# A deformable-convolution block on one core: the half-partition shift of the sampled rows, issued by GpSimd instead of by the sync engine

## What is computed

```python
x = x + _L0_conv_ref(_gn(x), ...)   # offsets, bilinear sampling, 3x3 convolution
x = x + _L1_conv_ref(_gn(x), ...)   # a depthwise 3x3 convolution whose taps come from the image's mean
```

## Time and profile before

| what | value |
|---|---|
| median of 3 runs | 1491.65 us |
| the profiled execution, its own time | 1493.54 us |
| its span, first to last instruction | 1491.7 us |
| TensorE busy (matmul) | 1436.3 us, 96% of the span |
| VectorE busy | 1257.4 us, 84% |
| ScalarE busy | 1152.9 us, 77% |
| GpSimd busy | 437.1 us, 29%, 474 instructions |
| mean granted TensorE clock | 0.992 |
| mean DMA rate | 207 GB/s |

### The profile page before, as it was taken

One profiled execution on the slowest core, in us unless ns is written; L12 is line 12 of the kernel. 1 busy time (PEld: TensorE's weight loads), 2 busy tenths in 40 slices (PEclk: granted clock), 3 DMA queues, 4 the chain that ended last, 5 costly groups with the idle time before them and its releaser, 6 DMA issues.

```text
span 1491.7 us, 30369 instructions
## 1 busy us (share of the span) xinstructions
PE 1436.3 (96%) x12300; PEld 617.9 (41%) x12300; DVE 1257.4 (84%) x884; ACT 1152.9 (77%) x1970; POOL 437.1 (29%) x474
## 2 busy tenths in 40 slices
PE   5898798999999999999999999999999999999978
PEld 2333343444444444444444444444444444444433
DVE  4999999988888898889888988888888889888900
ACT  6789687986888778887888877888688877766643
POOL 5000734225050432306141151412505043230120
PEclk9999999999999999999999999999999999999999
DMA  8576587977888788886979778897888877767558
GB/s 270 159 191 170 146 215 182 242 197 204 236 224 217 198 213 228 228 216 179 244 206 255 189 206 230 223 233 194 205 236 224 217 199 180 198 179 201 140 145 260
DMA packets 226907, 308.77 MB, mean 207 GB/s; under 512 B 17216, under 2 KB 169152, under 8 KB 226768
## 3 DMA queue, kind: packets, MB, share of 16 engines
q1 hardware_dynamic: 211360, 266.68, 61.2%
q0 software_dynamic: 15408, 40.15, 17.3%
HBM read 190.35 MB, written 38.14 MB: 153 GB/s over the span
## 4 chain that ended last, share of the span: by engine, by line
PE 89%; DVE 4%; DMA 2%; issue 2%; ACT 2%; POOL 1%; SPq 0%; DVEq 0%; ACTq 0%; POOLq 0%
PE z L402 46%; PE dc L442 24%; PE dw L475 14%; PE z L475 3%; DMA yr<-in_planes 1%; DVE nb L840 1%; DVE nb L838 1%; DMA yh<-yr 1%; DVE nb L818 1%; DVE nb L835 0%; PE dc L451 0%; ACT nb L635 0%; DVE nb L844 0%; DVE nb L842 0%; PE z L494 0%
## 5 line engine op out<-in xcount | busy, mean ns | idle before, releaser
L402 PE MATMUL z<-xv,wos 128*64 128x384 f32 x4608 | 766.1, 488 | 10.7 <-issue 7.6
L402 PEld LDWEIGHTS z<-xv,wos 128*64 128x64 f32 x4608 | 330.7, 137 | 429.8 <-issue 428.6
L442 PE MATMUL dc<-sr,wds 128*32 128x384 f32 x2304 | 396.4, 489 | 13.4 <-issue 9.5
L442 PE MATMUL dc<-sh,wds 128*32 128x384 f32 x2304 | 396.4, 489 | 0.0
L1017 POOL DMA_DIRECT2D yr<-in_xr x96 | 86.2, 898 | 767.1 <-ACT yr L669 767.1
L818 DVE COPY_PREDICATED nb<-mu,xv 128x2280 f32<-128x2280 uint16 x96 | 269.2, 2804 | 36.9 <-ACT mu L621 36.5
L442 PEld LDWEIGHTS dc<-sr,wds 128*32 128x32 f32 x2304 | 133.5, 108 | 237.2 <-issue 237.1
L475 PE MATMUL dw<-yh,wy 128*64 128x388 f32 x616 | 229.7, 494 | 0.0
L475 PE MATMUL dw<-yr,wy 128*64 128x388 f32 x616 | 229.7, 494 | 0.0
L635 ACT ACTIVATE nb<-xv 128x2292 f32<-128x2292 f32 x96 | 202.9, 2113 | 28.8 <-DVE sr L851 20.6
L614 ACT ACTIVATE du<-z,ob 128x768 f32<-128x768 f32 x96 | 86.4, 900 | 128.8 <-PE z L402 128.2
(11 more groups left out here) (130 smaller groups left out, 1594.6 us busy)
## 6 DMA issues: line engine op xcount, KB each, us to landing
xv<-in_x SPq DMA_DIRECT2D x272, 384.0 KB, 5.6
yr<-in_xr POOLq DMA_DIRECT2D x96, 392.0 KB, 5.0
out<-ot SPq DMA_DIRECT2D x96, 388.0 KB, 3.9
yh<-yr SPq DMA_DIRECT2D x178, 196.0 KB, 3.9
st<-in_planes SPq DMA_DIRECT2D x56, 576.0 KB, 7.5
sh<-sr SPq DMA_DIRECT2D x160, 194.0 KB, 5.1
sh<-sr SPq DMA_DIRECT2D x32, 145.5 KB, 5.7
yr<-in_planes SPq DMA_DIRECT2D x8, 576.0 KB, 10.3
```

Of the source, the lines that this page charges most:

```text
L402: last = nc.tensor.matmul(acc[m], weights[:, kx, :], view[:, :, kx:kx + W], start=kx == 0, stop=kx == 2)
L442: last = nc.tensor.matmul(dc[m, q, 0:NB * PAIRS], weights[:, kx, q], view[:, :, cols], start=first, stop=final)
```

## The change

`s_shift` moves, line for line, from the sync engine's program to GpSimd's; every `sp.` in it becomes `pool.`. In step i it is called behind `add_residual(i - 4)` and ahead of everything else that GpSimd does in the step. The last one, `s_shift(LAST)`, stands between the residuals of chunks 92 and 93. Transfers, sizes, semaphores and waited values are the same.

```diff
-            def s_shift(n):
...
-                sp.wait_ge(sampled, n + 1)
...
-                if i:
-                    s_shift(i - 1)
                 if b + 1 < B and o < STILES:
                     st_load(b + 1, o)
...
-            s_shift(LAST)
...
+            def s_shift(n):
+                b, j = divmod(n, CHUNKS)
+                k, done = s_at(n), s_sh[n % SS]
+                pool.wait_ge(sampled, n + 1)
+                pool.wait_ge(s_pads, SS * b + min(j + 1, SS))
+                wait(pool, dcn_mm, 2 * (n - 2))
+                lo, hi = slice(0, P // 2), slice(P // 2, P)
+                pool.dma_start(sh[lo, k:k + NB, :], sr[hi, k:k + NB, :]).then_inc(done, 16)
...
+                elif k == 0:
+                    pool.dma_start(sh[hi, SS * NB - 1, :], sr[lo, 0, :]).then_inc(done, 16)
+                    pool.dma_start(sh[hi, 0:NB - 1, :], sr[lo, 1:NB, :]).then_inc(done, 16)
+                else:
+                    pool.dma_start(sh[hi, k - 1:k + NB - 1, :], sr[lo, k:k + NB, :]).then_inc(done, 16)
...
                 if i > DCN_STEP:
                     add_residual(i - DCN_STEP - 1)
+                if i:
+                    s_shift(i - 1)
                 if o == 0:
...
-            for n in range(LAST - DCN_STEP, TOTAL):
+            add_residual(LAST - DCN_STEP)
+            s_shift(LAST)
+            for n in range(LAST - DCN_STEP + 1, TOTAL):
                 add_residual(n)
```

More of the change, by code:

```diff
@@ L305, in st_load @@
                 sp.dma_start(st[i % 2][:], planes[b, i]).then_inc(st_in[i % 2], 16)
-            def s_shift(n):
-                b, j = divmod(n, CHUNKS)
-                k, done = s_at(n), s_sh[n % SS]
-                sp.wait_ge(sampled, n + 1)
[L311 to L327, removed]
             def y_shift(n):
@@ L1011, in y_weights @@
                    tap[:].unsqueeze(2).to_broadcast([P, TAPS, CQ]), ALU.mult).then_inc(wy_ok, 1)
+            def s_shift(n):
[6 more added lines that the diff above has]
+                pool.dma_start(sh[lo, k:k + NB, :], sr[hi, k:k + NB, :]).then_inc(done, 16)
+                if j == 0:
+                    pool.dma_start(se[hi, b % 2, :], sr[lo, k, :]).then_inc(se_in[b % 2], 16)
+                    pool.dma_start(fe[2 * C:3 * C, b % 2, :], sr[0:C, k, :]).then_inc(done, 16)
+                    pool.dma_start(sh[hi, k:k + NB - 1, :], sr[lo, k + 1:k + NB, :]).then_inc(done, 16)
+                elif k == 0:
[3 more added lines that the diff above has]
+                    pool.dma_start(sh[hi, k - 1:k + NB - 1, :], sr[lo, k:k + NB, :]).then_inc(done, 16)
+                if j == CHUNKS - 1:
+                    pool.wait_ge(se_in[b % 2], 16 * (b // 2 + 1))
+                    pool.dma_start(sh[hi, k + NB - 1, :], se[hi, b % 2, :]).then_inc(done, 16)
+                    pool.dma_start(fe[C:2 * C, b % 2, :], sr[P - C:P, k + NB - 1, :]).then_inc(done, 16)
             def add_residual(n):
```

## The result

The changed kernel takes **1538.38 us** (median of 4 runs, 1537.56 to 1539.45); the kernel before took 1492.28 beside it. The ratio is 1.0307, with an interval from 1.0291 to 1.0322: 46.1 us slower. 1524.0 was forecast, within 1502 to 1540.

What follows compares the result with a forecast made beforehand. TensorE, busy nearly throughout, was taken as the bound, so each new wait on GpSimd's small arithmetic is lost time. 15.3 + 3.0 + 14.4 = 32.7 us more gave 1524 us, range 1502 to 1540.

Steps and rivals of the forecast that it cites:

- steps 10 and 16: `x_norm` of the second image and `y_norm` of the first: `hidden` of the first image comes 15.3 us later.
- step 18, `y_weights`: `y_weights` of the first image, behind `blend(17)` and two transfers: 3.0 us, bounds 0 and 4.8.
- six times `y_norm`: `y_norm` in images 3 to 8: `hidden` waits 2.4 us each time, 14.4 us in all; bounds 0.5 and 4.2 each.
- the clock: TensorE's granted clock behind the waits of steps 10 and 16: same loss on both sides, plus or minus 2 us.
- places put at 0: `x_norm` and `y_weights` of later images and the edge transfers: covered by about half a step, so 0 us.
- one turn more: Upper bound at `y_weights` of the first image: GpSimd's arithmetic waits out one further VectorE instruction, 4.8 us.
- so the price of issuing does not matter: Images 3 to 8: three transfers are through at 771.3, inside line 818, which runs until 772.45.
- rival 1: Images 3 to 8: GpSimd slips through VectorE's pauses, 0.5 us per image instead of 2.4; 1513 us, chance 0.22.
- GpSimd at its own pace: GpSimd's arithmetic, started late, is not held up by VectorE; 1492 us, no change, chance 0.08.
- the later images do not stall: Same claim as rival 1: 0.5 us per image instead of 2.4 in images 3 to 8; 1513 us, chance 0.22.
- Descriptors held up, too: Each shift transfer on GpSimd also waits for one VectorE instruction; 95.7 us more, 1587 us, chance 0.08.
- Faster: Shifts may land sooner from GpSimd's queue, and TensorE's 3.9 us of waits for them go; 1488 us, chance 0.04.

Runs made afterwards that it cites:

- Experiment 1: The changed kernel with the shift issued by GpSimd behind everything else in its step; 1496.77 us, ratio 1.0038.
- experiment 6: The changed kernel with four products of zeros on TensorE ahead of `hidden` in the six later images; 1532.92 us, ratio 1.0267.
- Experiment 2: The kernel before, shift still on SP, with only the wait for the sampled rows added on GpSimd behind the residual; 1518.50 us, ratio 1.0176.
- Experiments 3: The changed kernel with the shift behind `y_norm` in the fifth step of each image, from the second image on; 1525.62 us, ratio 1.0224.
- 4: The changed kernel with the shift behind `x_norm` and the next chunk's pads at o = 10; 1537.88 us, ratio 1.0311.
- 10: GpSimd issues shifts last in the step (at o = 4 right behind `y_norm`), but the last shift is given back to SP; 1495.82 us, ratio 1.0017.
- 9: GpSimd issues shifts last in the step (at o = 4 right behind `y_norm`), with chunk 93's residual ahead of the last shift; 1500.49 us, ratio 1.0051.
- experiment 7: The changed kernel with the shift last in GpSimd's step, but at o = 4 right behind `y_norm`, ahead of the pads; 1497.29 us, ratio 1.0031.

## Why the prediction was right, and where it fell short

**Right: the mechanism.** The change costs GpSimd little and puts a wait ahead of small arithmetic that TensorE and VectorE want. Experiment 1 shows it with the same transfers and the same wait, and nothing left to stand behind them in the step; the timelines show one operation per VectorE instruction in step 10 and in five of the six later images. Term by term, the forecast beside the trace (waits less those of the earlier trace rows):

| term | forecast | measured, from |
|---|---|---|
| steps 10 and 16 | 15.3 (its rows give 15.2) | 15.8: (16.2 - 7.6) + (11.8 - 4.6) |
| step 18, `y_weights` | 3.0 | 4.7, the wait at `y_bias` |
| six times `y_norm` | 14.4 | 12.0: five of 2.3, one of 0.5 |
| the clock | 0, plus or minus 2 | 9.4: 1071.8 - 1062.4, images 3 to 8 |
| places put at 0, the tail | 0 | 2.4: 44.7 - 42.3 |
| sum | 32.7 | 44.3, of 44.7 in the span |

The two terms of the first image's places leave out two things that nearly cancel. Up to the end of `blend(23)` TensorE is busy for 315.6 us instead of 312.8, 2.8 more, and its waits for shifted tiles are 2.7 us shorter.

**Mis-sized: the clock.** The text had "adds no third of that length, so I take the same loss on both sides, plus or minus 2 us". It looked only at waits as long as those of the earlier trace rows. The runs show that 2.3 us of idling are enough, in four of five images. From n = 23 to 95 the same instructions take 9.4 us more, and experiment 6, which keeps TensorE busy, leaves 0.7 of them; that 0.7 stays open. That 1538.4 still lies in the range, below 1540, is luck in this term: the top was room kept for other terms, 25.2 us for `y_norm` alone, which took 12.0.

**Step 18** came out at its upper bound, "one turn more". Line 978 of GpSimd, and VectorE beside it:

```profile
288.29 2.03 POOL L978 TENSOR_SCALAR tap<-tap,ry 128x16 f32<-128x16 f32 x1
```

```profile
288.26 1.07 DVE L800 COPY_PREDICATED xv<-mv,xv 128x768 f32<-128x768 uint16 x1
289.22 1.00 DVE L801 COPY_PREDICATED nb<-mv,nb 128x768 f32<-128x768 uint16 x1
```

Line 801 begins before line 800 is shown to end, and the operation waits out both: 290.32 against 290.22. This is not a rule. The same two lines stand as close in step 40 (line 800 until 620.39, line 801 from 620.28), and there line 940 ends between their ends, at 620.78. What decided it in step 18 is not shown.

**Right by an argument that was too coarse: "so the price of issuing does not matter"**, said of images 3 to 8. Between my two bounds, 0.63 and 0.95 us, it does not. Experiment 2 shows that at no price at all the first operations of `y_norm` slip in ahead of line 818 and the waits all but vanish, so rival 1 would have come true there. In the changed kernel it did come true in the last of the six images, with 0.5 us.

**The places put at 0** (edges, `x_weights`) did not show in the changed kernel. Experiments 3, 4 and 10 show that they were covered narrowly: when an earlier wait goes, they are next. **The tail** was not costed: the last shift moved ahead of a residual, and the forecast had no term for that.

**The rivals.** *GpSimd at its own pace* falls with step 10's timeline, *the later images do not stall* with the five waits of 2.3 us. *Descriptors held up, too* falls with the 0.53 us between transfers beside line 793 (163.25, 163.78, 164.29). The Trainium skill's rule behind it (SBUF — State Buffer, SBUF: two separate sides) speaks of a VectorE instruction that holds both ports; as far as these transfers go, no run here shows one. *Faster* was wrong on the total but right that waits for shifted tiles would shrink, from 13.4 us to 8.2. The prediction read only 3.9 us as such waits, because the profile puts the others down to "issue". What shrank them is not shown; a shorter landing it is not, as the page's transfers by line show, which answer to the earlier trace rows:

```profile
sh<-sr POOLq DMA_DIRECT2D x160, 194.0 KB, 6.3
```

## What to carry to other kernels

A transfer that is cheap to issue can still be expensive to move: list what stands behind its wait on the new engine, and who waits for each of those. When one place is mended, ask which wait was hidden by it, for here the next one took over four times (experiments 1, 3, 4 and 9). And a TensorE that is busy all the time should be costed with more than its idle time: read the granted clock behind each new wait.

## What the runs showed of the hardware

- 2.3 us of idling, after more than a hundred microseconds without any, were followed by the 1.2 GHz level in four of five images, and so were the 2.8 and 2.9 us in the tails of experiment 7 and the changed kernel. The kernel before idled 2.5 us in its tail, from 1423.07 on, with the clock at 1.00 behind it (1425 to 1432), and in experiment 2, with waits of 0.5 us at most in these images, the clock stayed at 1.00 behind those at 445, 623 and 801 us. With TensorE kept at work by products that nobody uses, it stayed at 1.00, and the kernel was 5.5 us faster.
- A shift takes 6.3 us to land in the changed kernel and 5.1 in the kernel before, but it is not GpSimd's queue in itself that makes it late: from the same queue, at a later place in the step, it takes 4.7 us in experiment 1, 4.5 in experiments 7 and 9 and 4.6 in experiment 10. What makes the 6.3 is not shown.
- In the tail, the last transfer of the last shift lands later when a residual has been issued ahead of it, whichever engine issues the shift: 5.1 us from SP in the kernel before, 4.8 from SP in experiment 10 and 6.2 from GpSimd in experiment 9, against 2.5 in experiment 7, where no residual was ahead. The Trainium skill (DMA: Bandwidth & Descriptors, Issuing engines are not separate DMA queues) says that all issuers feed the same 16 transfer engines, so that a second issuer saves little; these landings agree with it. What a second issuer did save is waiting to be issued: from SP the shift started 0.02 us behind the end of `blend(95)` (experiment 10), from GpSimd, behind the residual and its wait for ScalarE, 1.5 us behind it (experiment 9).
